# A conditioned attention block on one core: low parts of q and k made by GpSimd from a second eviction, two products of y at later slots

## The chip, the core and the metric

One Trainium2 chip, one of its cores, one launch. Times are microseconds of device time of that core. The kernel before takes 348.88 us (median of three runs, 348.82 to 350.72). TensorE multiplies, VectorE (DVE), ScalarE (ACT) and GpSimd (POOL) do elementwise work, and SyncE (SP) issues most DMAs; each runs its own stream of instructions in order, and they meet at semaphores.

## What is computed

Sixteen batches of 256 tokens with 256 features, sixteen heads of 16:

```python
h = _sln(hidden, w, ln_g, ln_b, Wg, bg, Wb, bb)       # gamma * LayerNorm + beta, gamma and beta from w
qkv = (h @ Wqkv.T + bqkv).reshape(B, N, num_heads, hd, 3)
energy = jnp.einsum('bhqd,bhkd->bhqk', q, k)
att = jax.nn.softmax(energy, axis=-1) / D ** 0.5
out = jnp.einsum('bhqk,bhkd->bhqd', att, v)
out = out @ Wp.T + bp
h1 = out + hidden
h2 = _sln(h1, w, ln_g, ln_b, Wg, bg, Wb, bb)
return h2 + h1
```

## The kernel before, in words

All products run as fp32r. To keep accuracy, an operand is split into a high part (rounded on eviction) and a low part (what the rounding lost), and a product is the sum of three: high by high, low by high, high by low. So q and k of a batch each exist twice in SBUF, as `qk_h` and `qk_l`, and SP's DMAs stack both in the partitions of `qst` and `kst`, so that one 128-deep matmul gives a head's full score.

**Steps and slots.** The work is pipelined over batches. Step b (b = -1 to 14) has 16 slots, one for each head h. In slot h TensorE makes the transposed scores of batch b (`scores`, tile st, two matmuls) and the scores of batch b + 1 from which only the row maxima are wanted (`scores_max`, tile sa, two matmuls). ACT takes the exponential of st into p (L602). DVE takes the row maxima of sa into mx (`maximum`, L688). Two banks each of st and sa alternate: `scores(b, h)` waits for the exponential of slot h - 2, `scores_max(b + 1, h)` for the maxima of slot h - 2. Between the scores stand, by slots that a table of constants at the top of the file gives, the projections of q and k of batch b + 2 (into banks m0 and m1, slots 0 to 6), v of b + 1 (m0, slots 7 and 8), the output projection of b - 1 (m1, slots 12 to 15), the products with v (`weigh`, 32 short matmuls, at slot 10 for heads 0 to 7 and at slot 2 of the next step for heads 8 to 15), and transposes. What is left after step 14 (the last scores, the last output) is written out as `last_step` and `finish`.

**The transpose of the maxima.** At slot 1 `transpose_max(b, 1, pv_ps[0])` (L1072) turns the maxima of heads 8 to 15 and writes into bank pv_ps[0]. That bank held the weighted values of heads 0 to 7, so TensorE first waits for `att_ready`, which DVE gives with `normalise(b - 1, 0, 1)` (L711, tile att), the last thing that DVE does in a step: the table `between` of DVE's `step` puts `normalise(b, 0, 0)` (L707, a reciprocal) in front of the maxima of slot 15 and `normalise(b, 0, 1)` behind them. In that table a key is (slot, side): side 0 stands in front of that slot's maxima, side 1 behind them.

**q and k.** ACT evicts the high parts: `high_q` in slot 5 (L522, two instructions of 128x256) and `high_k` in slot 7 (L532). DVE makes the low parts by `low_qk` (L723, two instructions for q behind the maxima of slot 5, two for k behind those of slot 7) straight from the PSUM bank: bank plus bias minus high part. `ql_ready` and `kl_ready` tell SP that the low parts may be sent and tell TensorE that the banks m0 and m1 are free again. Only for batch 1, in the first step, ACT writes a second, unrounded eviction (`full`, L631) into a free part of p32, and GpSimd subtracts (`low_full`, L415).

**The second LayerNorm.** `residual(b - 2, stage)` on DVE, stages 0 to 5: the sum h1, its statistics, and two products of y. Stage 4 (L804) is (h1 - mean) times gamma, stage 5 (L812) is that times rstd plus `h1b`; each is two instructions of 128x256 whose tensor inputs both lie in SBUF. GpSimd makes h1b (`add_beta`, L396), and adds the bias of the output projection to x for the next batch (`add_bias`, L387: xa plus bias_b, both in SBUF). `y_ready` releases SP's DMA of the output.

**GpSimd in a step**: DMAs of the negated maxima into qst (`maxima`, slots 3 and 11), a power for rstd (L430, slot 5), the normalisation of x for b + 3 (`norm_x`, L378, slot 5), `add_beta` (slot 6), the low part of h for b + 3 (`low_h`, L410, slot 12), then `add_bias` (slot 0 of the next step). It has no barrier at a slot; each instruction runs as soon as its semaphores allow.

**SP in a step**: the stack of b + 1, second half of the heads; x of b + 4; the stack of b + 2, first half (`send`: q high, q low, k high, k low, two DMAs each); gamma and beta of b - 1; the output of b - 2. `scores_max` waits for a stack at slots 0 and 8.

The functions that the change touches and what calls them:

Of the kernel before, what the change touches and what calls it, by code (L numbers as in the profile page):

```python
# [44 lines left out]
Q_SLOTS, K_SLOTS, V_SLOTS, P_SLOTS = (0, 1, 3, 4), (4, 5, 5, 6), (7, 7, 8, 8), (12, 13, 14, 15)  # L45
S_MT1, S_AT, S_MT0, S_XT = 1, 10, 9, 10
S_QH, S_KH, S_VH = 5, 7, 9
WARM = (10, 4, 4, 4)
V_FIRST = ((4, 5, 6, 6), (9, 10, 11, 12))
X_FIRST = 8  # L50
# [7 lines left out]
def cond_block(nc, x, condT, vectors, WgT, WbT, WqkvT, WpT, bp, out):  # L58
    gb_dram = nc.dram_tensor("gb_rows", (B, 2 * D), F32, kind="Internal").ap()
    with ExitStack() as ctx:  # L60
# [81 lines left out]
        stack_in = [[sem(f"stack_in{g}{p}") for p in range(2)] for g in range(2)]  # L142
        max_in = [[sem(f"max_in{g}{p}") for p in range(2)] for g in range(2)]
        max_first = sem("max_first")
        full_ready = sem("full_ready")
        qpad_ready = sem("qpad_ready")
        kpad_ready = sem("kpad_ready")
        y_out = [sem("y_out0"), sem("y_out1")]
# [207 lines left out]
        def _(pool):  # L356
# [54 lines left out]

            def low_full(a, t, ready):

                pool.wait_ge(full_ready, t + 1)
                pool.tensor_tensor(qk_l[:, par(a), t].rearrange("p g n -> p (g n)"), p32[:, H - 2 + t, :],  # L415
                                   qk_h[:, par(a), t].rearrange("p g n -> p (g n)"), ALU.subtract).then_inc(ready, 1)

            def step(b):
                for h in range(H):
                    if h == 5 and has(b):  # L420

                        one, two = has(b + 3), has(b - 2)
                        if one:
                            wait(pool, v_step, 3 * (b + 3) + 3)
                            wait(pool, xn_ready, 1 * (b + 3))
                        if two:
                            wait(pool, ln2_step, 4 * (b - 2) + 3)
                            wait(pool, y_ready, 1 * (b - 2))
                        which = slice(0 if one else 1, 2 if two else 1)
                        pool.tensor_tensor(rstd[:, which], vare[:, which], minus_half[:, which],  # L430
                                           ALU.pow).then_inc(rstd_ready, 1)
                    if first(b + 1) and h == 0:
                        low_full(1, 0, ql_ready)
                    if first(b + 1) and h == 5:
                        rstd_x(2)
                        low_full(1, 1, kl_ready)
                        norm_x(2)
                        pool.wait_ge(wph_ready, 1)
                        pool.tensor_tensor(wp_l[:], wp[:], wp_h[:], ALU.subtract).then_inc(wpl_ready, 1)
                    if h == 3:  # L440
                        maxima(b, 1)
                    if h == 11 and has(b):
                        maxima(b + 1, 0)
                    if h == 6 and has(b - 2):
                        add_beta(b - 2)
                    if h == 5 and has(b + 3) and has(b):
                        norm_x(b + 3)
                    if h == 0 and has(b - 1):
                        add_bias(b - 1)
                    if h in (13, 14) and b == B - 2:  # L450
                        add_bias(b + h - 13)
                    if h == 12:
                        low_h(b + 3)
# [42 lines left out]
        def _(act):  # L496
# [29 lines left out]
            def high_k(a):  # L526
# [6 lines left out]
                                             ACT.Identity, bias=vecs[:, 5, g:g + 1])  # L533
                o.then_inc(kh_ready, 1)

            def high_v(a, ps):

                wait(act, v_done, 1 * a + 1)
                wait(act, pv_done, 2 * (a - 1))
                nc.scalar.activation(v_st[:, par(a), :, :, 0:HD],  # L540
                                     ps[:].rearrange("p (t h d) -> p t h d", t=TT, h=H),
                                     ACT.Copy).then_inc(v_ready, 1)
# [9 lines left out]
            def step(b):  # L552
                for h in range(H):
# [5 lines left out]
                        high_q(b + 2)  # L559
                    if h == S_KH and not first(b + 1):  # L560
                        high_k(b + 2)
                    if h == S_MT1 + 1 and has(b):
                        high_max(b, 1, pv_ps[0])
                    if h == S_MT0 + 1 and has(b + 1):
# [60 lines left out]
                    act.dma_start(raw(kst[r:P:P // HD, 0, 0:HH, :]),  # L625
                                  raw(qk_h[:, 0, 1, 0, :])).then_inc(stack_in[0][0], 16)

            def full(a, t, ps):

                for g in range(KT):  # L630
                    o = nc.scalar.activation(p32[:, H - 2 + t, g * N:(g + 1) * N], ps[:, g * N:(g + 1) * N],  # L631
                                             ACT.Identity, bias=vecs[:, 4 + t, g:g + 1])
                o.then_inc(full_ready, 1)

            for dst, src, landed in ((wg, WgT, wg_in), (wb, WbT, wb_in)):
                act.dma_start(dst[:], src.rearrange("(k p) n -> p k n", p=P)).then_inc(landed, 16)
# [43 lines left out]
        def _(dve):  # L680
# [169 lines left out]
            def step(b):  # L850
# [5 lines left out]
                    (4, 0): [lambda: residual(b - 2, 2), lambda: norm1(b + 3, 0)],  # L856
                    (4, 1): [lambda: residual(b - 2, 3), lambda: norm1(b + 3, 1)],
                    (5, 0): [lambda: norm1(b + 3, 2)],
                    (5, 1): [lambda: low_qk(b + 2, 0, m0, qh_ready, ql_ready)],
                    (7, 0): [lambda: normalise(b - 1, 1, 0)],  # L860
                    (7, 1): [lambda: low_qk(b + 2, 1, m1, kh_ready, kl_ready)],
                    (8, 0): [lambda: normalise(b - 1, 1, 1)],
                    (9, 1): [lambda: residual(b - 2, 4)],
                    (11, 0): [lambda: low_max(b + 1, 0), lambda: low_att(b - 1), lambda: residual(b - 2, 5)],
                    (15, 0): [lambda: normalise(b, 0, 0)],
                    (15, 1): [lambda: normalise(b, 0, 1)],
                }
                if first(b + 1):
                    for slot in ((4, 0), (4, 1), (5, 0), (5, 1), (7, 1), (11, 0)):
                        del between[slot]  # L870
                    between[(9, 0)] = [lambda: low_max(0, 0)]
                for h in range(H):
# [94 lines left out]
        def _(pe):  # L967
# [278 lines left out]
            def step(b):  # L1246
                for h in range(H):
# [3 lines left out]
                    if h == (X_FIRST if first(b + 1) else S_XT) and has(b + 3):  # L1251
                        if has(b - 1):
                            wait(pe, v_ready, 1 * (b + 1) + 1)
                        elif has(b):
                            wait(pe, ql_ready, 1 * (b + 2) + 1)
                        else:
                            pe.wait_ge(full_ready, 1)
                        turn_x(b + 3)
                    if h == S_AT and has(b - 1):
                        turn_att(b - 1)  # L1260
# [17 lines left out]
                    for quarter in [n for n in range(4) if K_SLOTS[n] == h and has(b + 2) and not first(b + 1)]:  # L1278
                        if quarter == 0:
                            wait(pe, h1_ready, 1 * (b - 2) + 1)  # L1280
                            wait(pe, kl_ready, 1 * (b + 1) + 1)
                        project_qk(b + 2, 1, m1, k_done, quarter)
                    if h == S_MT0 and has(b + 1):
                        wait(pe, h1_ready, 1 * (b - 2) + 1)
                        wait(pe, kl_ready, B if not has(b + 2) else 1 * (b + 2) + 1 if has(b) else 1)
                        if first(b + 1):
                            pe.wait_ge(bias_ready, 1)
                        transpose_max(b + 1, 0, pv_ps[1] if first(b + 1) else m1)
                    for quarter in [n for n in range(4) if V_SLOTS[n] == h and has(b + 1) and has(b - 1)]:
                        if quarter == 0:  # L1290
                            wait(pe, ql_ready, (1 * (b + 2) + 1) if has(b + 2) else B)
                            wait(pe, v_ready, 1 * b + 1)
                        project_v(b + 1, m0, quarter)
                    for quarter in [n for n in range(4) if P_SLOTS[n] == h and has(b - 1)]:
                        if quarter == 0 and first(b - 1):
                            pe.wait_ge(wpl_ready, 1)
                        if quarter == 0:
                            wait(pe, aTl_ready, 1 * (b - 1) + 1)
                            wait(pe, h1_ready, 1 * (b - 2) + 1)
                            wait(pe, kl_ready, (1 * (b + 2) + 1) if has(b + 2) else B)  # L1300
                            wait(pe, ml_ready, 2 * min(b + 1, B - 1) + 1)
                        project_out(quarter)
                    if h < 4 and first(b + 1):
# [73 lines left out]
```

## Time and profile before

| | before |
|---|---|
| median of 3 runs | 348.88 us (348.82 to 350.72) |
| the profiled execution | 349.5 us, of which the span of its instructions is 347.7 us |
| busy: PE, PEld, DVE, ACT, POOL | 334.0, 288.6, 297.0, 242.8, 159.0 us |
| share of the span | 96%, 83%, 85%, 70%, 46% |
| DMA | 48.87 MB, mean 141 GB/s |
| granted TensorE clock, mean | 0.99 |
| chain that ended last | PE 86%, DVE 5%, ACT 2%, DMA 2%, POOL 2% |

PE is the matmul side of TensorE and PEld its loading of weights, which overlaps. Busy time of PE is modelled and matmuls are pipelined, so a busy PE says that something was always in flight, not that nothing waits. Lines such as L688 are lines of the kernel before.

### The profile page before, as it was taken

Reading aid. Unit: us, or ns where it says so; the run is one execution under the profiler, and the core shown is the slowest. Engines: PE = TensorE matmul, PEld = TensorE weight load, DVE = VectorE, ACT = ScalarE, POOL = GpSimd, SP = SyncE. Lnnn points to the kernel's source line nnn. Section 1 sums busy time; section 2 is a strip of 40 time slices with the busy share of each in tenths; the row PEclk is TensorE's granted clock in tenths of the full one; section 3 lists DMA queues with packets and bytes.
Section 4 is the critical chain, followed back from the end, with each engine's and each line's share of the span. In section 5 each row is a group of like instructions: output and inputs, shape, how many; then the busy total and the mean of one; then the engine's idle time right before and its main releaser. Section 6 shows DMA issues by size and latency. Waiting matters only on the chain.

```text
span 347.7 us, 8982 instructions
## 1 busy us (share of the span) xinstructions
PE 334.0 (96%) x3173; PEld 288.6 (83%) x3173; DVE 297.0 (85%) x728; ACT 242.8 (70%) x476; POOL 159.0 (46%) x187
## 2 busy tenths in 40 slices
PE   8886989999999999999999999999999999999993
PEld 4675968889898888888898888888898888888773
DVE  4874877789898989989898989989898988998684
ACT  7762686868678686868687686868687686766740
POOL 5476261525464462726454462726454453225330
PEclk9997899999999999999999999999999999999999
DMA  8487245544555465565545565656546454652011
GB/s 239 128 202 204 58 123 151 150 134 129 161 131 158 135 180 155 136 173 139 157 133 156 134 176 153 141 154 160 156 135 154 106 170 124 168 147 75 18 60 60
DMA packets 47705, 48.87 MB, mean 141 GB/s; under 512 B 6287, under 2 KB 41374, under 8 KB 47662
## 3 DMA queue, kind: packets, MB, share of 16 engines
q1 hardware_dynamic: 44782, 47.00, 49.3%
q0 software_dynamic: 1984, 0.51, 0.9%
q10 hardware_dynamic: 896, 0.80, 0.8%
q8 instruction: 25, 0.41, 0.5%
q14 instruction: 18, 0.15, 0.1%
HBM read 9.99 MB, written 4.23 MB: 41 GB/s over the span
## 4 chain that ended last, share of the span: by engine, by line
PE 86%; DVE 5%; ACT 2%; DMA 2%; POOL 2%; issue 2%; SPq 0%; DVEq 0%; POOLq 0%; ACTq 0%
PE m L969 24%; PE st L969 19%; PE sa L969 18%; PE pv L969 17%; PE pv L1058 4%; PE pv L1139 2%; PE m L1098 2%; DMA wqkv<-WqkvT_dram 2%; DVE mx L688 1%; DVE qk_l L723 1%; POOL qk_l L415 1%; POOL xn L378 1%; PE pv L1072 1%; PE m L1072 1%; ACT qk_h L522 0%
## 5 line engine op out<-in xcount | busy, mean ns | idle before, releaser
L688 DVE TENSOR_REDUCE mx<-sa 128x2 f32<-128x512 f32 x256 | 171.6, 683 | 30.1 <-PE sa L969 29.0
L602 ACT ACTIVATE p<-st 128x512 f32<-128x512 f32 x240 | 140.9, 598 | 38.0 <-PE st L969 33.9
L969 PE MATMUL sa<-kst,qst 126*128 126x256 f32 x512 | 106.5, 290 | 1.6 <-DVE mx L688 1.1
L969 PE MATMUL st<-qst,kst 128*128 128x256 f32 x496 | 104.0, 292 | 0.7 <-DMA qst<-m_l 0.5
L969 PEld LDWEIGHTS st<-qst,kst 128*128 128x128 f32 x496 | 75.1, 188 | 14.3 <-issue 12.8
L969 PEld LDWEIGHTS sa<-kst,qst 126*128 126x128 f32 x512 | 80.0, 193 | 3.8 <-DVE mx L688 2.1
L369 POOL DMA_DIRECT2D qst<-m_h x31 | 17.6, 566 | 117.0 <-DVE m_l L697 117.0
L969 PE MATMUL pv<-p,v_st 128*32 128x256 f32 x1008 | 61.0, 382 | 0.0
L969 PEld LDWEIGHTS pv<-p,v_st 128*32 128x32 f32 x1008 | 29.5, 109 | 21.0 <-ACT p L602 1.8
L969 PE MATMUL m<-hT_h,wqkv_h 128*128 128x256 f32 x128 | 36.8, 300 | 1.4 <-issue 0.8
L378 POOL TENSOR_SCALAR xn<-xa,mv,rstd 128x256 f32<-128x256 f32 x28 | 34.2, 1227 | 1.4
L969 PE MATMUL m<-hT_h,wqkv_l 128*128 128x256 f32 x128 | 34.4, 280 | 0.4 <-DVE wqkv_l L909 0.4
L969 PE MATMUL m<-hT_l,wqkv_h 128*128 128x256 f32 x128 | 34.2, 279 | 0.0
L430 POOL TENSOR_TENSOR rstd<-vare,minus_half 128x4 f32<-128x4 f32 (+1 forms) x15 | 14.2, 947 | 40.4 <-DVE vare L745 36.3
L550 ACT ACTIVATE oT<-pv 128x512 f32<-128x512 f32 x29 | 17.2, 594 | 21.6 <-PE pv L969 21.6
L723 DVE SCALAR_TENSOR_TENSOR qk_l<-m,vecs,qk_h 128x256 fp32r<-128x256 f32 x60 | 25.9, 473 | 0.6 <-ACT qk_h L522 0.6
L969 PEld LDWEIGHTS m<-hT_h,wqkv_h 128*128 128x128 f32 x128 | 23.5, 189 | 2.3 <-ACT wqkv_h L642 1.2
L969 PEld LDWEIGHTS m<-hT_h,wqkv_l 128*128 128x128 f32 x128 | 23.6, 190 | 0.6 <-DVE wqkv_l L909 0.6
L969 PEld LDWEIGHTS m<-hT_l,wqkv_h 128*128 128x128 f32 x128 | 23.4, 187 | 0.0
L396 POOL TENSOR_TENSOR h1b<-h,gb 128x512 f32<-128x512 f32 x15 | 19.3, 1289 | 6.9 <-DVE h L784 6.9
L387 POOL TENSOR_TENSOR xa<-xa,bias_b 128x512 f32<-128x512 f32 x16 | 20.6, 1292 | 0.0
L410 POOL TENSOR_TENSOR hT_l<-hT,hT_h 128x512 fp32r<-128x512 f32 x14 | 18.0, 1289 | 4.0 <-ACT hT_h L503 4.0
(149 smaller groups left out, 568.3 us busy)
## 6 DMA issues: line engine op xcount, KB each, us to landing
qst<-qk_h SPq DMA_DIRECT2D x64, 128.0 KB, 2.4
qst<-qk_l SPq DMA_DIRECT2D x64, 128.0 KB, 2.5
kst<-qk_l SPq DMA_DIRECT2D x64, 128.0 KB, 2.7
kst<-qk_h SPq DMA_DIRECT2D x62, 128.0 KB, 2.4
xa<-x_dram SPq DMA_DIRECT2D x16, 256.0 KB, 3.0
gb<-gb_rows SPq DMA_DIRECT2D x16, 256.0 KB, 3.9
out_dram<-y SPq DMA_DIRECT2D x15, 256.0 KB, 3.4
wqkv<-WqkvT_dram SPq DMA_DIRECT2D x1, 512.0 KB, 5.8
```

The source lines that it names most:

```text
L369: pool.dma_start(raw(qst[MAX_ROW + r:MAX_ROW + 1 + r, p, g * HH:(g + 1) * HH, :]) .rearrange("a h (t n) -> a (h t) n", t=TT), raw(m[:, g, ...
L378: o = pool.tensor_scalar(xn[:, t, :], xbuf(a)[:, t, :], mv[:, t, 0:1], rstd[:, 0, t:t + 1], ALU.subtract, ALU.mult)
L387: pool.tensor_tensor(xbuf(a), xbuf(a), bias_b[:].rearrange("p (a n) -> p a n", a=1).broadcast_to([P, TT, D]), ALU.add).then_inc(xdb_ready, 1)
L396: pool.tensor_tensor(h1b[:], h1[:], gb[:, par(a), D:2 * D].rearrange("p (a n) -> p a n", a=1) .broadcast_to([P, TT, D]), ALU.add).then_inc ...
L410: pool.tensor_tensor(hT_l[:, par(a)], hT[:], hT_h[:, par(a)], ALU.subtract).then_inc(hTl_ready, 1)
L430: pool.tensor_tensor(rstd[:, which], vare[:, which], minus_half[:, which], ALU.pow).then_inc(rstd_ready, 1)
L550: nc.scalar.activation(oT[:, g, :], pv_ps[g][:], ACT.Copy).then_inc(oT_ready, 1)
L602: nc.scalar.activation(p32[:, h, :], st_ps[h % 2][:], ACT.Exp).then_inc(exp_done, 1)
L688: dve.tensor_reduce(mx[:, par(a), h // HH, (h % HH) * TT:(h % HH + 1) * TT], sa_ps[h % 2][:].rearrange("p (t n) -> p t n", t=TT), AX.X, AL ...
L723: o = dve.scalar_tensor_tensor(out=qk_l[:, par(a), t, g, :], in0=ps[:, g * N:(g + 1) * N], scalar=vecs[:, 4 + t, g:g + 1], in1=qk_h[:, par ...
L969: return nc.tensor.matmul(o, l, r, start=start, stop=stop)
L1058: o = nc.tensor.transpose(pv_ps[g][:, t * N + c * P:t * N + (c + 1) * P], oT[:, g, c * N + t * P:c * N + (t + 1) * P], ident[:])
```

## The change

The low parts of q and k of all batches from 2 on are now made as those of batch 1 were. ACT evicts each bank a second time, unrounded and with its bias, q in slot 6 and k in slot 8, into `wg` and `wb` (weights that nothing reads after the set-up). GpSimd subtracts the high part from it: `low_full` of q at slot 6, behind `norm_x`; of k at slot 9; `add_beta` goes from slot 6 to slot 7 and so stands between the two. The four instructions of `low_qk` in each step leave DVE. The waits for the banks m0 and m1 are now for the second eviction (`fq_ready`, `fk_ready`) and no longer for the low part. Of the products of y, stage 4 goes from behind the maxima of slot 9 to behind those of slot 13, stage 5 from in front of slot 11 to behind slot 14.

```diff
+S_QF, S_KF = 6, 8
...
             def low_full(a, t, ready):
 
-                pool.wait_ge(full_ready, t + 1)
-                pool.tensor_tensor(qk_l[:, par(a), t].rearrange("p g n -> p (g n)"), p32[:, H - 2 + t, :],
+                if not has(a):
+                    return
+                pool.wait_ge((fq_ready, fk_ready)[t], 1 * a)
+                pool.tensor_tensor(qk_l[:, par(a), t].rearrange("p g n -> p (g n)"),
+                                   (wg, wb)[t][:].rearrange("p g n -> p (g n)"),
                                    qk_h[:, par(a), t].rearrange("p g n -> p (g n)"), ALU.subtract).then_inc(ready, 1)
...
-                    if h == 6 and has(b - 2):
+                    if h == 6 and has(b):
+                        low_full(b + 2, 0, ql_ready)
+                    if h == 7 and has(b - 2):
                         add_beta(b - 2)
+                    if h == 9 and has(b):
+                        low_full(b + 2, 1, kl_ready)
...
+            def full(a, t, ps):
+
+                if not has(a):
+                    return
+                wait(act, (ql_ready, kl_ready)[t], 1 * a)
+                for g in range(KT):
+                    o = nc.scalar.activation((wg, wb)[t][:, g, :], ps[:, g * N:(g + 1) * N],
+                                             ACT.Identity, bias=vecs[:, 4 + t, g:g + 1])
+                o.then_inc((fq_ready, fk_ready)[t], 1)
...
+                    if h == S_QF and not first(b + 1):
+                        full(b + 2, 0, m0)
+                    if h == S_KF and not first(b + 1):
+                        full(b + 2, 1, m1)
...
-                    (5, 1): [lambda: low_qk(b + 2, 0, m0, qh_ready, ql_ready)],
                     (7, 0): [lambda: normalise(b - 1, 1, 0)],
-                    (7, 1): [lambda: low_qk(b + 2, 1, m1, kh_ready, kl_ready)],
                     (8, 0): [lambda: normalise(b - 1, 1, 1)],
-                    (9, 1): [lambda: residual(b - 2, 4)],
-                    (11, 0): [lambda: low_max(b + 1, 0), lambda: low_att(b - 1), lambda: residual(b - 2, 5)],
+                    (11, 0): [lambda: low_max(b + 1, 0), lambda: low_att(b - 1)],
+                    (13, 1): [lambda: residual(b - 2, 4)],
+                    (14, 1): [lambda: residual(b - 2, 5)],
                     (15, 0): [lambda: normalise(b, 0, 0)],
                     (15, 1): [lambda: normalise(b, 0, 1)],
...
                         if quarter == 0:
                             wait(pe, h1_ready, 1 * (b - 2) + 1)
-                            wait(pe, kl_ready, 1 * (b + 1) + 1)
+                            wait(pe, fk_ready, 1 * (b + 1))
                         project_qk(b + 2, 1, m1, k_done, quarter)
...
                         if quarter == 0:
-                            wait(pe, ql_ready, (1 * (b + 2) + 1) if has(b + 2) else B)
+                            wait(pe, fq_ready, min(b + 2, B - 1))
                             wait(pe, v_ready, 1 * b + 1)
                         project_v(b + 1, m0, quarter)
```

The transpose of the maxima at slot 9 into m1 and the output projection likewise wait for `fk_ready` where they waited for `kl_ready`.

What stands in a row on DVE, from the maxima of slot 10 to those of slots 0 to 2 of the next step. Before:

```order
L697 SCALAR_TENSOR_TENSOR m_l<-m,m_h 16x128
L773 TENSOR_TENSOR aT_l<-pv,aT_h 128x512
L812 SCALAR_TENSOR_TENSOR y<-y,rstd,h1b 128x256 x2
L688 TENSOR_REDUCE mx<-sa 128x2 x4
L707 RECIPROCAL rec<-pv 128x16
L688 TENSOR_REDUCE mx<-sa 128x2
L711 TENSOR_TENSOR att<-pv,rec 128x2x128
L688 TENSOR_REDUCE mx<-sa 128x2 x3
```

The four maxima (mx<-sa) in a row are those of slots 11 to 14, the one behind rec that of slot 15. The same place after the change (lines are those of the changed file; L705 is the maxima, L724 rec, L728 att):

```order
L714 SCALAR_TENSOR_TENSOR m_l<-m,m_h 16x128
L790 TENSOR_TENSOR aT_l<-pv,aT_h 128x512
L705 TENSOR_REDUCE mx<-sa 128x2 x3
L821 SCALAR_TENSOR_TENSOR y<-h,mv,gb 128x256 x2
L705 TENSOR_REDUCE mx<-sa 128x2
L829 SCALAR_TENSOR_TENSOR y<-y,rstd,h1b 128x256 x2
L724 RECIPROCAL rec<-pv 128x16
L705 TENSOR_REDUCE mx<-sa 128x2
L728 TENSOR_TENSOR att<-pv,rec 128x2x128
```

Both pairs of y now stand between the maxima of slot 13 and the att of the step's end; before, neither did.

GpSimd through one step, from the power for rstd to the bias of x. Before:

```order
L430 TENSOR_TENSOR rstd<-vare,minus_half 128x4
L378 TENSOR_SCALAR xn<-xa,mv,rstd 128x256 x2
L396 TENSOR_TENSOR h1b<-h,gb 128x512
L369 DMA qst<-m_h 1x16x128
L369 DMA qst<-m_l 1x16x128
L410 TENSOR_TENSOR hT_l<-hT,hT_h 128x512
L387 TENSOR_TENSOR xa<-xa,bias_b 128x512
```

The same stretch after the change:

```order
L435 TENSOR_TENSOR rstd<-vare,minus_half 128x4
L380 TENSOR_SCALAR xn<-xa,mv,rstd 128x256 x2
L419 TENSOR_TENSOR qk_l<-wg,qk_h 128x512
L398 TENSOR_TENSOR h1b<-h,gb 128x512
L419 TENSOR_TENSOR qk_l<-wb,qk_h 128x512
L371 DMA qst<-m_h 1x16x128
L371 DMA qst<-m_l 1x16x128
L412 TENSOR_TENSOR hT_l<-hT,hT_h 128x512
L389 TENSOR_TENSOR xa<-xa,bias_b 128x512
```

Two subtractions of 128x512 have come in ahead of the DMAs of the maxima, the low part of h and the bias of x.

## Rows read from the trace of the kernel before

**Rows 1.** Busy time by engine in two consecutive stretches of 19.5 us, with instruction counts

```profile
131.95:151.45 19.50, 19.50 (x197) 17.29 (x196) 17.84 (x45) 14.58 (x30) 9.37 (x10) 1.00 0.54 151
151.45:170.95 19.50, 19.50 (x197) 17.29 (x196) 17.84 (x45) 14.58 (x30) 9.38 (x10) 1.00 0.54 152
```

**Rows 2.** The chain that ended last, one piece in step 0: start, us, what

```profile
42.84 0.78 DVE qk_l L723 x2
```

**Rows 3.** Groups by line and shape: count, busy us, mean ns, idle before

```profile
L602 ACT ACTIVATE p<-st 128x512 f32<-128x512 f32 x240 | 140.9, 598 | 38.0 <-PE st L969 33.9
...
L723 DVE SCALAR_TENSOR_TENSOR qk_l<-m,vecs,qk_h 128x256 fp32r<-128x256 f32 x60 | 25.9, 473 | 0.6 <-ACT qk_h L522 0.6
...
L415 POOL TENSOR_TENSOR qk_l<-p,qk_h 128x512 fp32r<-128x512 f32 x2 | 2.6, 1294 | 1.9 <-ACT p L631 1.9
...
L631 ACT ACTIVATE p<-m,vecs 128x256 f32<-128x256 f32 x4 | 1.7, 480 | 0.0
```

**Rows 4.** Timeline of DVE, slots 9 to 15 of one step: start, us, instruction

```profile
162.53 0.87 DVE L804 SCALAR_TENSOR_TENSOR y<-h,mv,gb 128x256 f32<-128x256 f32 x2
163.32 0.68 DVE L688 TENSOR_REDUCE mx<-sa 128x2 f32<-128x512 f32 x1
...
166.02 2.01 DVE L688 TENSOR_REDUCE mx<-sa 128x2 f32<-128x512 f32 x3 [0.42 <-PE sa L969]
168.20 0.69 DVE L688 TENSOR_REDUCE mx<-sa 128x2 f32<-128x512 f32 x1 [0.17 <-PE sa L969]
168.81 0.24 DVE L707 RECIPROCAL rec<-pv 128x16 f32<-128x16 f32 x1
169.47 0.69 DVE L688 TENSOR_REDUCE mx<-sa 128x2 f32<-128x512 f32 x1 [0.42 <-PE sa L969]
170.08 0.41 DVE L711 TENSOR_TENSOR att<-pv,rec 128x256 f32<-128x256 f32 x1
```

**Rows 5.** Timeline of PE, slot 1 of the step after it

```profile
170.69 0.40 PE L969 MATMUL sa<-kst,qst 126*128 126x256 f32 x2
170.92 0.28 PE L1072 MATMUL pv<-ident,mx 128*128 128x128 f32 x1
```

**Rows 6.** Timelines of POOL and DVE: two additions of POOL, one pair of L804

```profile
167.00 1.29 POOL L387 TENSOR_TENSOR xa<-xa,bias_b 128x512 f32<-128x512 f32 x1
...
337.24 1.27 POOL L491 TENSOR_TENSOR xn<-xa,gb 128x512 f32<-128x512 f32 x1
...
338.13 1.06 DVE L804 SCALAR_TENSOR_TENSOR y<-h,mv,gb 128x256 f32<-128x256 f32 x2
```

**Rows 7.** Timelines of POOL, ACT and PE within the same step

```profile
158.85 2.44 POOL L378 TENSOR_SCALAR xn<-xa,mv,rstd 128x256 f32<-128x256 f32 x2
...
164.49 0.61 POOL L369 DMA_DIRECT2D qst<-m_h  x1 [1.95 <-DVE m_l L697]
...
159.11 0.84 ACT L532 ACTIVATE qk_h<-m,vecs 128x256 fp32r<-128x256 f32 x2 [0.45 <-PE m L969]
...
161.74 0.48 PE L969 MATMUL st<-qst,kst 128*128 128x256 f32 x2
162.07 0.50 PE L969 MATMUL sa<-kst,qst 126*128 126x256 f32 x2
```

**Rows 8.** DMA issues: x count, KB each, median us from issue to landing

```profile
kst<-qk_l SPq DMA_DIRECT2D x64, 128.0 KB, 2.7
```

**Rows 9.** Timelines at the ends of steps 13 and 14: DVE, PE, POOL

```profile
302.07 2.00 DVE L688 TENSOR_REDUCE mx<-sa 128x2 f32<-128x512 f32 x3
306.60 0.31 PE L1072 MATMUL pv<-ident,mx 128*128 128x128 f32 x1
...
319.13 1.99 DVE L688 TENSOR_REDUCE mx<-sa 128x2 f32<-128x512 f32 x3
...
319.16 2.54 POOL L387 TENSOR_TENSOR xa<-xa,bias_b 128x512 f32<-128x512 f32 x2
...
323.16 0.41 DVE L711 TENSOR_TENSOR att<-pv,rec 128x256 f32<-128x256 f32 x1
```

More of the change, by code:

```diff
@@ L144, in cond_block @@
         max_first = sem("max_first")
-        full_ready = sem("full_ready")
+        fq_ready = sem("fq_ready")
+        fk_ready = sem("fk_ready")
         qpad_ready = sem("qpad_ready")
@@ L626, in high_k0 @@
                                   raw(qk_h[:, 0, 1, 0, :])).then_inc(stack_in[0][0], 16)
[L628 to L633, printed above, removed]
             for dst, src, landed in ((wg, WgT, wg_in), (wb, WbT, wb_in)):
@@ L868, in step @@
                 if first(b + 1):
-                    for slot in ((4, 0), (4, 1), (5, 0), (5, 1), (7, 1), (11, 0)):
+                    for slot in ((4, 0), (4, 1), (5, 0), (11, 0)):
                         del between[slot]
@@ L1254, in step @@
                         elif has(b):
-                            wait(pe, ql_ready, 1 * (b + 2) + 1)
+                            wait(pe, fq_ready, 1 * (b + 2))
                         else:
-                            pe.wait_ge(full_ready, 1)
+                            pe.wait_ge(fq_ready, 1)
                         turn_x(b + 3)
@@ L1284, in step @@
                         wait(pe, h1_ready, 1 * (b - 2) + 1)
-                        wait(pe, kl_ready, B if not has(b + 2) else 1 * (b + 2) + 1 if has(b) else 1)
+                        if has(b):
+                            wait(pe, fk_ready, min(b + 2, B - 1))
+                        else:
+                            pe.wait_ge(kl_ready, 1)
                         if first(b + 1):
@@ L1299, in step @@
                             wait(pe, h1_ready, 1 * (b - 2) + 1)
-                            wait(pe, kl_ready, (1 * (b + 2) + 1) if has(b + 2) else B)
+                            wait(pe, fk_ready, min(b + 2, B - 1))
                             wait(pe, ml_ready, 2 * min(b + 1, B - 1) + 1)
```

## Prediction

> **What bounds the kernel now.** I read the views in this order. First the busy time of each engine in two stretches that lie exactly one step apart: both are 19.50 us, with the same 197 matmuls, PE busy for all of 19.50 and DVE for 17.84 [rows 1]. So the middle of the run repeats to the hundredth, its period is 19.50 us, and the engine without a gap is TensorE. Second the chain of waits that ended last: it is 86% PE, and DVE's work on q and k shows in it as a piece of the first full step, 42.84 us [rows 2]. Third, for the change, the groups by line, which give the price of each operation [rows 3], and last the timelines, which say who is how far behind whom at the two places where work comes and goes. What the reader should see before any sum: with TensorE the bound, work taken off DVE gives back only what TensorE now loses waiting for DVE, which in the steady part is next to nothing, while work put in front of something that TensorE waits for costs from the point where its slack is used up.
>
> **That slack, at the end of a step.** At slot 1 TensorE transposes the maxima into the bank that DVE's last product of the step (att, L711) still reads. att starts at 170.08 and takes 0.41, so it ends at 170.49 [rows 4]; the transpose starts at 170.92 [rows 5]. The slack is 0.43 us. DVE gets there from the three maxima of slots 11 to 13, which end at 168.03; then it waits 0.17 for the scores of slot 14 and 0.42 for those of slot 15 [rows 4], so 0.59 of idle time also lies in this stretch.
>
> **Part 1: y moved to slots 13 and 14.** Two pairs of 128x256 products come into this stretch. A pair takes 0.87, and the next instruction starts 0.79 after it (162.53 to 163.32); a maximum passes on after 0.61 (168.20 to 168.81), because an instruction starts about 0.08 before the one ahead of it has ended, so the reciprocal of 0.24 passes on after 0.16 [rows 4]. New times, in the frame of that step: the maxima of slots 11 to 13 end at 168.03 as before, since they wait for TensorE; stage 4 starts at 167.95, the maxima of slot 14 at 168.74, stage 5 at 169.35, the reciprocal at 170.14, the maxima of slot 15 at 170.30, att at 170.91, and att ends at 171.32. There is no wait left between them. With 0.05 us for the semaphore (an estimate; bounds 0 and 0.1) the transpose starts at 171.37 in place of 170.92: 0.45 us later. A part of these 0.45 us TensorE already loses one instruction earlier: its scores for the maxima of slot 1, at 170.69 [rows 5], need the maxima of slot 15, which end at 170.99, so 0.35 is waited there and the other 0.10 at the transpose; they don't add. DVE is level with TensorE again by slot 11, in front of whose maxima it stands idle for 0.42 [rows 4], so the delay is paid once per step and does not pile up.
>
> **A slower stage 4.** Stage 4 now starts at 167.95, and GpSimd's addition of the bias to x ran at 167.00 to 168.29 before [rows 6]. It moves later: two subtractions of 1.29 [rows 3] go in between norm_x, which ends at 161.29, and the DMAs of the maxima; they pass on after some 1.26 each, 2.5 in all, and GpSimd was idle for 1.95 in front of the first DMA [rows 7], which leaves 0.55; behind the DMAs it waits for ACT's hT_h, where a little more can be made up, so I take the addition to start 0.4 later, at 167.4, and to end at 168.7. It overlaps stage 4 by 0.75 (by 0.34 if it didn't move, by 0.87 at the most). What an overlap costs the trace shows once: the pair of L804 at 338.13 took 1.06 in place of 0.87, and a GpSimd addition ran until 338.51, so of 0.38 us beside it 0.19 were lost [rows 6]. At that rate 0.75 costs 0.37; the bounds are 0 and 0.43. The stall becomes 0.45 + 0.37 = 0.82 us.
>
> The Trainium skill (GPSIMD Engine Reference, Key points) says that GpSimd shares its SBUF interfaces with VectorE and that it contends with DVE instructions that have two SBUF inputs. Stage 4 has two (h1 and gamma), the maxima and low_qk have one or none in SBUF; the one pair at 338.13 agrees. By this rule the result is the forecast below, without it the first rival.
>
> **How often.** Stages 4 and 5 run in steps 2 to 14. For the 11 steps 2 to 12 the stall is 0.82: 9.0 us. Step 13: GpSimd has neither norm_x nor the low part of h there, so its addition is over before; the maxima end at 304.07, and the same sums (0.79, 0.61, 0.79, 0.16, 0.61, 0.41, less the first 0.08) end att at 307.36, against a transpose that started at 306.60 [rows 9]: 0.81. Step 14: the maxima end at 321.12, additions run on GpSimd until 321.70, so stage 4 loses 0.33, and att ends at 324.74 where it ended at 323.57 and was already waited for [rows 9]: 1.17. Together 11.0 us.
>
> **Part 2: low_qk off DVE.** 56 instructions (14 batches of 4, the other 4 of the 60 are batch 0's) of 0.473 leave: 26.5 us of DVE [rows 3], all beside a busy TensorE except in step 0, where they are on the chain: two pairs, 1.6 us at the most [rows 2]. There the same step gets ACT's second evictions and later DMAs, and TensorE's own work is close behind; I take 0.5 us of gain, bounds 0 and 1.6. In the steady steps TensorE's pair for the maxima of slot 10 takes 0.50 against 0.40 elsewhere [rows 5, 7], which I read as a wait of 0.1 for DVE; it goes: at the most 12 times 0.1 = 1.2 us.
>
> **Part 3: the second eviction on ACT.** 56 instructions of 0.48 [rows 3], 27 us, four in a step. ACT has gaps, but not everywhere. From 159.11 it evicts k (0.84) [rows 7], then comes exponential 7 (0.60) [rows 3], then the new pair (0.84, as k's), then exponential 8 (0.60). Less 0.11 by which one starts inside the one before (two of 0.473 take 0.84), exponential 8 ends at 161.66, and TensorE's scores of slot 10, which wait for it, start at 161.74 [rows 7]. That is just in time. Without overlaps it would be 161.99 and cost 0.3 a step, 3.6 us; I take 0.05 a step against the 0.1 won above, net -0.05 times 12 = -0.6 us (bounds -1.2 and +3.6).
>
> **Part 4: the subtractions on GpSimd.** 28 of 1.29 [rows 3], 36 us, on an engine that is half idle. Behind them wait SP's DMAs of the low parts. q's ends at about 162.6, k's at 165.1, so the last two DMAs of the stack are issued from 165.1; the second leaves an issue later, some 0.6 (GpSimd's own issue in rows 7 takes 0.61), and lands 2.7 after that, at 168.4 [rows 8]. TensorE wants it at slot 0 of the next step, not before 169.5 (170.69 less a slot, 19.5/16). 1.1 us spare: cost 0. SP's output DMA now waits for stage 5 until about 170.6, and the second half of the next stack is queued behind it, about 1 us later than before; it is wanted at slot 8: cost 0.
>
> **The sum** is made against the profiled execution: 349.5 + 11.0 - 0.5 - 0.6 = 359.4 us, 9.9 more. That execution is 0.6 above the median of 348.88, so on the median: 358.8 us.
>
> **The rivals.**
> - No contention: stage 4 beside GpSimd's addition is no slower. For it: the evidence is one pair. Then 11 times 0.45 + 0.81 + 0.84 - 1.1 = 5.5, 354.4 us.
> - DVE is relieved and nothing is lost. The mechanism: DVE is 3.2 us a step lighter ahead of the maxima of slot 11 (two pairs of q and k, two of y, 0.79 each), arrives early at slot 14, and att still ends before TensorE needs its bank. It decides at one point, att's end against 170.87. Then the gains stand alone: 1.2 + up to 1.6, so 346.1 to 348. Against it: the maxima of slots 11 to 13 wait for TensorE, so being early doesn't carry over [rows 4].
> - GpSimd late: if its subtractions run 2 us later than worked out, the low part of k lands after slot 0 is due, by more than the 0.82 that are lost anyway, and each further 0.5 us costs 12 times 0.5: about 365. The idle stretch of 1.95 speaks against it.
> - ACT late at slot 10 by the full 0.3: 0.35 more in 12 steps, 363.0.
>
> **How the numbers follow.** Chances: forecast 0.58, no contention 0.22, GpSimd late 0.04, ACT late 0.06, relief 0.10 (of it 0.03 for faster by over 1%, since its best price is 0.8%, and 0.07 for within 1%). One per cent is about what a measurement of this kernel tells from no change. Slower by over 1%, above 352.4: 0.90. The range takes in the first rival with 1 us below it and the forecast with most of ACT's bound above: 353.5 to 362.5.
>
> **What would show it.** In the changed profile: a period of 20.2 to 20.3 us (19.50 + 0.82 - 0.05); a new wait of TensorE at the slot 1 transpose for DVE's att and at slot 1's scores for the maxima of slot 15; pairs of L804's successor at about 1.2 us and of L812's at 0.87; no DVE idle time between slots 13 and 15. A period of 19.95 with pairs of 0.87 would be the first rival. It is wrong if the period stays at 19.5, or if TensorE's new waits stand elsewhere: at slot 0 for a DMA, at slot 10 for ACT.

## The result, and the profile after

The changed kernel takes 361.56 us (median of 4 runs, 360.82 to 362.39) against 348.85 for the kernel before (4 runs): ratio 1.036, 95% interval 1.033 to 1.039. It is 12.7 us slower; 9.9 were forecast. The profiled execution took 362.23 us, with a span of 360.4.

The windows of two consecutive steps of the changed kernel, to be held against [rows 1] (columns: stretch, its length, then busy us and count of PE, PEld, DVE, ACT, POOL, the granted clock, the DMA share, GB/s):

```profile
147.67:168.10 20.43, 19.93 (x198) 17.37 (x202) 17.05 (x41) 15.78 (x33) 11.80 (x13) 1.00 0.52 145
168.10:188.53 20.43, 19.93 (x198) 17.37 (x202) 17.05 (x41) 15.78 (x33) 11.80 (x13) 1.00 0.54 145
```

The period has gone from 19.50 to 20.43 us, and PE is no longer busy throughout. DVE does less (17.05 after 17.84), ACT and POOL do more (15.78 after 14.58, 11.80 after 9.37). So DVE, the busiest engine behind TensorE, was relieved, and the step became longer all the same: the time went into waits.

Where, the timeline of DVE at the end of a step says, which answers to [rows 4]:

```profile
170.67 2.00 DVE L705 TENSOR_REDUCE mx<-sa 128x2 f32<-128x512 f32 x3 [1.21 <-PE sa L985]
172.59 1.47 DVE L821 SCALAR_TENSOR_TENSOR y<-h,mv,gb 128x256 f32<-128x256 f32 x2
173.99 0.68 DVE L705 TENSOR_REDUCE mx<-sa 128x2 f32<-128x512 f32 x1
174.59 0.87 DVE L829 SCALAR_TENSOR_TENSOR y<-y,rstd,h1b 128x256 f32<-128x256 f32 x2
175.38 0.24 DVE L724 RECIPROCAL rec<-pv 128x16 f32<-128x16 f32 x1
175.54 0.62 DVE L705 TENSOR_REDUCE mx<-sa 128x2 f32<-128x512 f32 x1
176.09 0.40 DVE L728 TENSOR_TENSOR att<-pv,rec 128x256 f32<-128x256 f32 x1
```

From the maxima of slots 11 to 13 to att nothing waits any more; the 1.21 us of idle time lie in front of the row and are of no use to it. Beside it POOL, and then PE at slots 0 and 1, which answer to [rows 6] and [rows 5]:

```profile
172.09 1.28 POOL L389 TENSOR_TENSOR xa<-xa,bias_b 128x512 f32<-128x512 f32 x1
```

```profile
174.26 0.39 PE L985 MATMUL st<-qst,kst 128*128 128x256 f32 x2
174.81 0.47 PE L985 MATMUL sa<-kst,qst 126*128 126x256 f32 x2 [0.16 <-DVE mx L705]
...
175.48 0.40 PE L985 MATMUL st<-qst,kst 128*128 128x256 f32 x2
176.22 0.51 PE L985 MATMUL sa<-kst,qst 126*128 126x256 f32 x2 [0.34 <-DVE mx L705]
176.56 0.31 PE L1088 MATMUL pv<-ident,mx 128*128 128x128 f32 x1
```

The rows before that these are held against, beside [rows 5]:

```profile
169.86 0.40 PE L969 MATMUL sa<-kst,qst 126*128 126x256 f32 x2
170.45 0.40 PE L969 MATMUL st<-qst,kst 128*128 128x256 f32 x2
```

A pair sa starts 0.24 after its pair st where nothing is waited for (170.45 and 170.69 before). Here it is 0.55 at slot 0 and 0.74 at slot 1, and the transpose comes 0.34 after it in place of 0.23: 0.31 + 0.50 + 0.11 = 0.92 us. What stands behind a late pair comes later too: from sa of slot 0 to the next st it is 0.67 (174.81 to 175.48) in place of 0.59 (169.86 to 170.45), and from the transpose to the weighing of slot 2 it is 1.07 in place of 1.03. So the stall is 1.04 us. It is more than the 0.93 of the period, because the step gets 0.12 back, 0.10 of it at TensorE's pair sa of slot 10, which took 0.50 before [rows 7] and is 0.40 now:

```profile
166.82 0.40 PE L985 MATMUL sa<-kst,qst 126*128 126x256 f32 x2
```

For the whole: 11 steps times 0.93 are 10.2 us. From transpose to transpose at slot 1, step 13 takes 19.37 (299.15 to 318.52; before 287.94 to 306.60, 18.66) and step 14 17.80 (318.52 to 336.32; before 17.03): 0.7 and 0.8. The other 1.1 lie in front of the first weighing of step 0, at 48.29 against 47.20 before. Nothing shows that they belong to the change: in executions whose programs are the same up to there the first weighing starts at 46.2 to 48.6 us (46.24 in e5_y_apart, 48.58 in e3_bias_late), which is a wider spread than 1.1.

### The profile page after: what moved, and what is told of

Read it like the earlier page. It is cut to its first block, busy times and chain, and to the rows that moved or that the text cites. A ratio compares the mean times of both kernels' runs of the same rounds, so it can differ in the third digit from the quotient of the medians.

```text
span 360.4 us, 8996 instructions
## 1 busy us (share of the span) xinstructions
PE 341.4 (95%) x3173; PEld 291.6 (81%) x3173; DVE 284.2 (79%) x672; ACT 259.6 (72%) x532; POOL 193.3 (54%) x215
## 4 chain that ended last, share of the span: by engine, by line
PE 70%; DVE 14%; issue 9%; ACT 3%; POOL 2%; DVEq 0%; POOLq 0%; ACTq 0%
PE m L985 18%; PE pv L985 17%; PE sa L985 15%; PE st L985 13%; DVE mx L705 6%; DVE y L821 3%; DVE y L829 3%; PE pv L1074 2%; PE m L1114 2%; PE pv L1155 2%; ACT p L625 1%; POOL qk_l L419 1%; ACT qk_h L531 1%; PE pv L1088 1%; POOL xn L380 1%
## 5 line engine op out<-in xcount | busy, mean ns | idle before, releaser
L705 DVE TENSOR_REDUCE mx<-sa 128x2 f32<-128x512 f32 x256 | 170.6, 683 | 45.7 <-PE sa L985 41.8
L985 PEld LDWEIGHTS sa<-kst,qst 126*128 126x128 f32 x512 | 79.1, 190 | 13.2 <-DVE mx L705 8.6
L985 PE MATMUL m<-hT_h,wqkv_h 128*128 128x256 f32 x128 | 37.6, 309 | 0.6 <-ACT hT_h L639 0.6
L985 PEld LDWEIGHTS m<-hT_h,wqkv_h 128*128 128x128 f32 x128 | 24.7, 201 | 1.6 <-issue 1.6
L419 POOL TENSOR_TENSOR qk_l<-wg,qk_h 128x512 fp32r<-128x512 f32 x15 | 19.4, 1290 | 1.5 <-ACT wg L551 1.5
L419 POOL TENSOR_TENSOR qk_l<-wb,qk_h 128x512 fp32r<-128x512 f32 x15 | 19.3, 1285 | 1.5 <-ACT wb L551 1.5
```

The lines of the kernel that those rows point to most:

```text
L705: dve.tensor_reduce(mx[:, par(a), h // HH, (h % HH) * TT:(h % HH + 1) * TT], sa_ps[h % 2][:].rearrange("p (t n) -> p t n", t=TT), AX.X, AL ...
L985: return nc.tensor.matmul(o, l, r, start=start, stop=stop)
```

## The experiments

Each kernel was timed beside the kernel before; the ratios are to that. "Late addition" below means GpSimd's addition of the bias to x moved from slot 0 to slot 3.

**e1_y_back.** The second part of the change undone:

```diff
+                    (9, 1): [lambda: residual(b - 2, 4)],
-                    (11, 0): [lambda: low_max(b + 1, 0), lambda: low_att(b - 1)],
-                    (13, 1): [lambda: residual(b - 2, 4)],
-                    (14, 1): [lambda: residual(b - 2, 5)],
+                    (11, 0): [lambda: low_max(b + 1, 0), lambda: low_att(b - 1), lambda: residual(b - 2, 5)],
```

> The changed kernel with the two products of y back at their old places (stage 4 behind the maxima of slot 9, stage 5 in front of slot 11); ACT's second eviction and GpSimd's subtractions stay. Theory (the whole loss is DVE's longer row in front of att at the end of a step): period 19.40 to 19.50 us, no wait of TensorE at slots 0 and 1, 348 to 350 us. The pair of stage 4 may still be slow (over 1.1 us in place of 0.87), since it now stands beside GpSimd's subtraction, but there it costs nothing. Rival (a part of the loss is the second eviction on ACT or the later low parts): period above 19.6, 352 us or more.

Measured: 366.18 us, ratio 1.050 (1.047 to 1.053), period 20.99. It is slower still, and by more than the rival expected. The expectation had foreseen that the pair of stage 4 could be slow here, but at no cost. The timelines of DVE, POOL and PE in one step:

```profile
167.67 2.96 DVE L821 SCALAR_TENSOR_TENSOR y<-h,mv,gb 128x256 f32<-128x256 f32 x2
170.55 0.68 DVE L705 TENSOR_REDUCE mx<-sa 128x2 f32<-128x512 f32 x1
171.15 0.27 DVE L714 SCALAR_TENSOR_TENSOR m_l<-m,m_h 16x128 fp32r<-16x128 f32 x1
171.35 0.67 DVE L790 TENSOR_TENSOR aT_l<-pv,aT_h 128x512 fp32r<-128x512 f32 x1
171.94 0.86 DVE L829 SCALAR_TENSOR_TENSOR y<-y,rstd,h1b 128x256 f32<-128x256 f32 x2
...
167.65 1.27 POOL L398 TENSOR_TENSOR h1b<-h,gb 128x512 f32<-128x512 f32 x1
168.88 1.47 POOL L419 TENSOR_TENSOR qk_l<-wb,qk_h 128x512 fp32r<-128x512 f32 x1
...
170.86 0.40 PE L984 MATMUL st<-qst,kst 128*128 128x256 f32 x2
171.28 0.50 PE L984 MATMUL sa<-kst,qst 126*128 126x256 f32 x2
172.07 0.39 PE L984 MATMUL m<-wp_h,aT_h 128*128 128x256 f32 x1 [0.29 <-DVE aT_l L790]
...
172.53 0.39 PE L984 MATMUL st<-qst,kst 128*128 128x256 f32 x2
173.46 0.50 PE L984 MATMUL sa<-kst,qst 126*128 126x256 f32 x2 [0.54 <-DVE mx L705]
```

The pair of stage 4 takes 2.96 us where it took 0.87. It runs beside h1b and the new subtraction until 170.35, 2.68 us, and loses 2.09. Behind it aT_l and the maxima come late, and TensorE waits at slots 12 and 13: sa starts 0.42 and 0.93 after its st in place of 0.24, and the output projection starts 0.79 after the first sa in place of 0.24 (166.07 to 166.31 before). These three make 1.42 of the 1.61 us by which the period exceeds 19.38. (One step in this trace took 22.39; there the DMA of the maxima landed 5.04 us after its issue, and the period is read from the others.) So the place of y in the kernel before is only good as long as GpSimd has nothing to do beside it; with the subtractions there, moving y gains 4.6 us (366.18 to 361.56).

**e2_y_only.** The kernel before with only the products of y moved (the same lines of the table as in the change, no second eviction, low_qk still on DVE).

> The kernel before with only the two products of y moved to behind slots 13 and 14; low parts of q and k stay on DVE. Theory: GpSimd's addition to x runs earlier than in the changed kernel (167.0 to 168.3 in the frame of the trace of before), overlaps stage 4 by some 0.3 us only, and costs some 0.25 us of it; with the 0.45 of the bare row the period is 20.1 to 20.2 us and the time 356 to 359 us. Rival (the loss comes mostly from ACT's and GpSimd's new work): under 354 us.

Measured: 357.14 us, ratio 1.026 (1.022 to 1.031), period 20.08. The time is as expected, the period at the lower edge, since stage 4 lost 0.14 and not 0.25. The pair and the addition beside it:

```profile
169.31 1.01 DVE L804 SCALAR_TENSOR_TENSOR y<-h,mv,gb 128x256 f32<-128x256 f32 x2
...
168.36 1.29 POOL L387 TENSOR_TENSOR xa<-xa,bias_b 128x512 f32<-128x512 f32 x1
```

They overlap by 0.34 us, and the pair loses 0.14.

**e3_bias_late.** The changed kernel with nothing of GpSimd beside stage 4:

```diff
-                    if h == 0 and has(b - 1):
+                    if h == 3 and has(b - 1):
                         add_bias(b - 1)
```

> The changed kernel with GpSimd's addition of the bias to x moved from slot 0 to slot 3, behind the DMAs of the maxima, so that nothing of GpSimd runs beside stage 4. Theory (contention of two instructions with two SBUF inputs each): the pair of stage 4 takes 0.87 us in place of 1.47, TensorE waits 0.4 us a step at slots 0 and 1 in place of 1.0, period 19.8 to 19.9, time 354.5 to 356 us. Rival (stage 4 is slow at that place for another reason, as SP's or GpSimd's DMAs): pair 1.4 us or more, 361 us.

Measured: 355.03 us, ratio 1.017 (1.014 to 1.021), period 19.83. The pair:

```profile
170.47 0.87 DVE L821 SCALAR_TENSOR_TENSOR y<-h,mv,gb 128x256 f32<-128x256 f32 x2
...
177.21 1.30 POOL L389 TENSOR_TENSOR xa<-xa,bias_b 128x512 f32<-128x512 f32 x1
```

One addition, moved on an engine that is half idle, takes 0.60 out of the period, all that the pair was too long. The contention is shown, and by its removal. In this trace one late transfer is hidden behind the row: in the step that ends at 154.02 the low part of k landed at 152.75 and TensorE's sa of slot 0 started 0.46 after its st.

**e4_y5_late.** The changed kernel with stage 4 back behind slot 9 and stage 5 behind slot 14.

> The changed kernel with stage 4 back behind slot 9 and only stage 5 behind slot 14. Theory (the row in front of att has 0.59 us of idle time and 0.43 of slack, which hold one pair of 0.79 but not two): att ends just before TensorE asks for its bank, period 19.40 to 19.55, time 348 to 350.5 us. Rival (any product of y in the row costs its own 0.79 us): period about 20.2, 357 us.

Measured: 362.41 us, ratio 1.040 (1.036 to 1.043), period 20.63. It told nothing of the row in front of att, since it has e1's fault: stage 4 took 2.96 us again, and stage 5 met the addition and took 1.40. e6 and e7 ask the same question without that.

**e5_y_apart.** Stage 4 beside norm_x, stage 5 where it was:

```diff
+                    (6, 1): [lambda: residual(b - 2, 4)],
-                    (11, 0): [lambda: low_max(b + 1, 0), lambda: low_att(b - 1)],
-                    (13, 1): [lambda: residual(b - 2, 4)],
-                    (14, 1): [lambda: residual(b - 2, 5)],
+                    (11, 0): [lambda: low_max(b + 1, 0), lambda: low_att(b - 1), lambda: residual(b - 2, 5)],
```

> The changed kernel with stage 4 of y behind slot 6, where GpSimd runs norm_x (one tensor input in SBUF), and stage 5 back in front of slot 11, after GpSimd's subtraction of k. Theory (only GpSimd instructions with two SBUF tensor inputs slow a product of y down; second evictions and subtractions cost nothing by themselves): the pair of stage 4 takes 0.87 to 0.95 us beside norm_x, stage 5 at most 1.3, period 19.40 to 19.50, 347 to 349 us, so no slower than before and perhaps 0.2% faster. Rival (anything that GpSimd does slows y): the pair of stage 4 takes 2 us or more, and TensorE waits for the maxima of slots 6 and 7: 355 us or more.

Measured: 354.58 us, ratio 1.015 (1.012 to 1.018). The period is 19.38, below that of the kernel before, as the theory had it; the total is not. (The profiled execution is one of the shorter ones, 352.59.) The pairs in a middle step, and then stage 5 in step 14:

```profile
163.19 1.34 DVE L829 SCALAR_TENSOR_TENSOR y<-y,rstd,h1b 128x256 f32<-128x256 f32 x2
...
176.87 1.01 DVE L821 SCALAR_TENSOR_TENSOR y<-h,mv,gb 128x256 f32<-128x256 f32 x2
...
318.50 3.77 DVE L829 SCALAR_TENSOR_TENSOR y<-y,rstd,h1b 128x256 f32<-128x256 f32 x2
```

```profile
162.58 1.28 POOL L419 TENSOR_TENSOR qk_l<-wb,qk_h 128x512 fp32r<-128x512 f32 x1
...
176.80 2.70 POOL L380 TENSOR_SCALAR xn<-xa,mv,rstd 128x256 f32<-128x256 f32 x2
...
319.06 2.52 POOL L389 TENSOR_TENSOR xa<-xa,bias_b 128x512 f32<-128x512 f32 x2
```

Beside norm_x, whose instructions have one tensor input, the pair loses only 0.14 in its whole length, and norm_x loses too (2.70 against the 2.44 of [rows 7]). In the last two steps GpSimd has no norm_x, so its later work comes beside stage 4 (in step 13 the subtraction of q and h1b, in step 14 h1b), and its additions beside stage 5, one in step 13 and two in step 14; there the pairs take 1.61 to 3.77 us, and steps 13 and 14 take 20.87 and 19.96 us where the kernel before needs 18.66 and 17.03. That is 5.1 us lost in two steps.

**e6_one_pair.** Stage 4 behind slot 6, stage 5 behind slot 14, late addition: one undisturbed pair in the row.

> The changed kernel with stage 4 behind slot 6, stage 5 behind slot 14 and GpSimd's addition of the bias at slot 3: one pair in the row in front of att, with nothing of GpSimd beside it. Theory: 0.59 us of idle time and 0.43 of slack hold the pair of 0.79, no wait of TensorE at slot 1, period 19.40 to 19.55, 347.5 to 350 us. Rival (each pair in the row costs what it takes): period about 20.2.

Measured: 350.80 us, ratio 1.004 (1.002 to 1.007), period 19.38, the last two steps 19.98 and 17.85. No wait at slot 1 in the middle steps: the row in front of att holds one pair. The total is 0.8 above what was expected: the last two steps, where stage 4 again meets the subtraction and h1b (2.51 us) or h1b alone (1.61), lose 1.3 and 0.8. Step 2 takes 19.81, because TensorE waits there at slot 0 for the low part of k.

**e7_before_y5.** The kernel before with only stage 5 behind slot 14.

> The kernel before with only stage 5 moved to behind slot 14; stage 4 stays behind slot 9. Theory: as with one pair in the changed kernel, the row holds it: period 19.40 to 19.55, 348 to 350 us. If the row had less room than worked out, the period is above 19.7 and the time above 351.

Measured: 349.75 us, ratio 1.003 (1.001 to 1.005), period 19.50, last two steps 18.90 and 17.29. The same answer without any other edit; only in steps 13 and 14, whose slack is smaller, some 0.25 us each are lost.

**e8_before_bias.** e2 with the late addition: both pairs in the row, undisturbed, without second eviction and subtractions.

> The kernel before with both products of y behind slots 13 and 14 and GpSimd's addition of the bias at slot 3; low parts stay on DVE. Theory (second eviction and subtractions cost nothing of their own): the same 19.80 to 19.87 us of period and 354 to 356 us as the changed kernel with the late addition. Rival (they have a cost of their own, from ACT at slot 10 or the late low parts): this kernel is faster than that one, by 1.5 us or more.

Measured: 354.86 us, ratio 1.017 (1.014 to 1.020), period 19.94. The time is as expected and the same as that of e3 (355.03), with a period 0.11 longer than e3's and 0.07 above what was expected. So at the places of the changed kernel ACT's second eviction and GpSimd's subtractions, together with the relief of DVE that they bring, cost nothing in a usual step; they gain 0.11. What they did use up is the time in hand of the low part of k. Its last transfer landed 2.3 to 3.7 us before TensorE's sa of slot 0 in the kernel before, over eleven steps of the middle, and 0.5 to 1.8 us before it in the changed kernel, where that sa is itself 0.3 late.

**e9_best.** e5, with the last steps as in e1, where both pairs had been undisturbed:

```diff
                     (6, 1): [lambda: residual(b - 2, 4)],
...
+                if b >= B - 3:
+                    between[(9, 1)] = between.pop((6, 1))
```

> The kernel with stage 4 behind slot 6 and stage 5 in front of slot 11, except that from step 13 on, where GpSimd has no norm_x and subtracts beside slot 6, stage 4 stands behind slot 9 again. Theory: both pairs are 0.87 us again in steps 13 and 14, these steps take 18.6 and 17.1 us in place of 20.9 and 20.0, the others 19.38 as they did; the time is 346.5 to 348.5 us, 0.1 to 0.6% below the kernel before. Rival (the rest of the 354.6 us has another cause than these two steps): 351 us or more.

Measured: 349.12 us (12 runs) against 349.30 (17 runs) for the kernel before on the same chip, ratio 0.997 (0.994 to 1.000). Steps 13 and 14 take 18.59 and 17.03 as expected, the others 19.38 but for one. The time itself is outside the expected range; the runs lie in two groups, 346.6 to 347.4 and 349.1 to 349.7, most likely because the starts differ between executions by more than the gain. The ratio is inside, but its interval reaches 1.000, so it is the period that shows the gain and not the time. Two windows of it:

```profile
132.26:151.64 19.38, 19.33 (x193) 16.98 (x193) 16.99 (x40) 15.65 (x34) 12.07 (x12) 1.00 0.51 138
151.64:171.02 19.38, 19.38 (x196) 17.22 (x195) 16.98 (x40) 15.32 (x34) 12.06 (x12) 1.00 0.58 166
```

In the second TensorE is without a gap again, now at 19.38. That is 0.12 us a step, 1.4 us in 12 steps, as far as these runs show all that relieving DVE gives here. In the first it has a short one. The chain of waits shows the transfer of the low part of k, and behind it TensorE's pair of slot 0:

```profile
148.44 2.62 DMA kst<-qk_l
...
151.10 0.51 PE sa L986 x2
```

That step, from transpose to transpose, takes 19.70. One step like it is in e5 (19.55) and in e6 (19.81). So with the low parts on GpSimd their transfer has next to nothing in hand, and now and then it costs 0.2 to 0.4 us.

**Six periods from the same terms.** Without these waits a step takes 19.38 us with the low parts on GpSimd and 19.50 with them on DVE. Two pairs of y in the row cost 0.45, as the forecast had it, and the contention comes on top. (e1 and e4, where stage 4 delays slots 12 and 13, are not of this form.)

| kernel | base | row | lost by stage 4 | sum | measured |
|---|---|---|---|---|---|
| changed kernel | 19.38 | 0.45 | 0.60 | 20.43 | 20.43 |
| e3_bias_late | 19.38 | 0.45 | 0 | 19.83 | 19.83 |
| e2_y_only | 19.50 | 0.45 | 0.14 | 20.09 | 20.08 |
| e8_before_bias | 19.50 | 0.45 | 0 | 19.95 | 19.94 |
| e6_one_pair | 19.38 | 0 (one pair) | out of the row | 19.38 | 19.38 |
| e7_before_y5 | 19.50 | 0 (one pair) | none | 19.50 | 19.50 |

## Why the prediction was right, and where it was off

**Right: the mechanism and its place.** TensorE had no gap, so that DVE's relief could give little; the slack in front of the transpose of slot 1 was 0.43 us, and two pairs of y overrun it. TensorE's new waits stand at slot 1, for the maxima and at the transpose, as foretold. A third, of 0.31 at slot 0 for the maxima of slot 14, was not in the forecast; it is there because stage 4, which stands in front of these maxima, took longer than was worked out, and in e3, without the contention, that pair starts 0.23 after its st (172.15 to 172.38).

**Right to a hundredth: 0.45 for the bare row.** e3 and e8 measure it alone: 19.83 less 19.38, 19.94 less 19.50. That it fits so closely is in part luck, since the 0.05 in it for the semaphore was a guess; from att's end to the transpose it is 0.07 here (176.49 to 176.56).

**Mis-sized: the slower stage 4.** The step that failed is "at that rate 0.75 costs 0.37; the bounds are 0 and 0.43". The overlap was right (0.78 us, 172.59 to 173.37), the rate was not: 0.60 were lost, beyond the bound. The rate came from one short meeting, 0.19 lost in 0.38 [rows 6]. The runs give, as overlap and loss: 0.34 and 0.14, 0.38 and 0.19, 0.67 and 0.47 (e5, stage 5), 0.71 and 0.54 (e4, stage 5), 0.78 and 0.60, 0.93 and 0.74 (e5, stage 4 of step 14). Where the pair meets one such instruction the loss is the overlap less 0.17 to 0.20, and not a share of it; 0.19 in 0.38 looked like half by accident of its length. The traces say it in another way too: a product of y that is slowed by an addition or subtraction of this kind ends 0.28 to 0.30 us after that instruction has ended, in every trace, however long the overlap was. In e1 both products of the pair meet one, hence 2.09 lost in 2.68. By this the forecast's own overlap of 0.75 would have cost 0.56. The upper bound was drawn from the same single point and so was no bound.

The stall was 1.05 in place of 0.82: 0.23 a step, 2.5 us over 11 steps. Against the profiled execution the forecast was 2.8 short, and the other terms make up the rest: the start, 1.25 us later at the transpose of step 0's slot 1 (39.27 after 38.02), was in no term; step 0 gained 0.35 less than was put; against these stand 0.8 more of gain in steps 1 to 12, and 0.1 and 0.4 less loss in steps 13 and 14. That the time is still in the range, 0.9 under its upper end, is luck: that end was set for a late ACT, which did not happen, and not for this term.

**The Trainium skill** (GPSIMD Engine Reference, Key points) was right in kind: contention with DVE instructions that have two SBUF inputs. The runs agree and put numbers to it, and they add that GpSimd's side matters: beside its instructions with one tensor input (norm_x) the loss is 0.14 us over the whole pair (1.01 us).

**Right in total, by too narrow an argument: parts 3 and 4 at nothing.** e3 against e8 shows that second eviction and subtractions cost nothing in a usual step at the places of the changed kernel. The 1.1 us in hand that the forecast gave the low part of k is in the middle of what is measured (0.5 to 1.8), but it was one step's figure: it differs from step to step, and in one step each of e5, e6 and e9 it is gone. But the forecast priced only what waits for the subtractions, and not what runs beside them: in e1 they cost 19.38 to 20.99, 1.6 us a step. So the move of y, which the forecast took as the sole cause of the loss, is at the same time what keeps the other half of the change from doing worse. The comparison "low parts moved, y left" stood in no part of the working.

**The small terms.** The gain at slot 10 was put at 0.1 a step with 0.05 given back by ACT; the period gains 0.12 with nothing given back (ACT's chain was in time, as worked out). Step 0 was put at 0.5 of gain. The chain of waits in it now reads

```profile
42.07 0.84 ACT qk_h L531 x2
42.91 0.49 ACT p L625
43.40 0.73 ACT wg L551 x2
44.13 0.49 ACT p L625
44.62 0.73 ACT qk_h L541 x2
45.35 0.49 ACT p L625
45.84 0.73 ACT wb L551 x2
46.57 0.50 ACT p L625
```

ACT has taken DVE's place on it: what q and k took off DVE in [rows 2] came back as two pairs of ACT, and the gain in this step is 0.15. Step 13 was put at 0.81 and is 0.7. Step 14 was put at 1.17 and is 0.8, since GpSimd's additions there ended just before stage 4 began, in place of running 0.66 into it:

```profile
332.96 0.87 DVE L821 SCALAR_TENSOR_TENSOR y<-h,mv,gb 128x256 f32<-128x256 f32 x2
...
330.31 2.56 POOL L389 TENSOR_TENSOR xa<-xa,bias_b 128x512 f32<-128x512 f32 x2
...
336.32 0.33 PE L1088 MATMUL pv<-ident,mx 128*128 128x128 f32 x1 [0.92 <-DVE att L728]
```

**The rivals.** No contention: refuted, e3 has the time that this rival gives. Relief of DVE and nothing lost: it is true of the middle steps of e5, e6 and e9, that is, where at most one pair is in the row and nothing slows stage 4; the point at which it decides, att's end, was the right one. GpSimd late: not in the changed kernel, and in one step each of e5, e6 and e9, at 0.2 to 0.4 us. ACT late: it did not show.

## What to carry to other kernels

Where one engine has no gap, a change to the others is priced by the slack in front of what it waits for, and idle time counts only if it lies inside the row between two meetings with that engine: here 1.21 us in front of the row were worth nothing, and 0.59 in it plus 0.43 behind it held one pair of 0.79 but not two. When work is given to GpSimd, look first at which DVE instructions with two inputs in SBUF run beside it, and only then at who waits for it. A price taken from a single meeting of two engines is a point and not a rate: two meetings of different length tell whether the loss is a share of the overlap or the overlap less a constant.

## What the runs showed of the hardware that was not expected

- A DVE instruction with two tensor inputs in SBUF stands still beside a GpSimd instruction of that kind, all but 0.17 to 0.20 us of a meeting: 0.60 lost in 0.78, and with two meetings 2.09 in 2.68, a pair of 128x256 products going from 0.87 to 2.96 us. GpSimd hardly notices (1.47 in place of 1.29 at the most). A meeting of only 0.10 us cost nothing (0.87 in e7 at 259.21). Beside a GpSimd instruction with one tensor input the same pair lost 0.14 in its whole length (e5). The maxima, whose input is in PSUM, and aT_l, with one input in each memory, kept their times beside the same GpSimd instructions (0.67 to 0.69).
- In step 14 of e5 the pair took 3.77 us, 2.90 more than alone, while the additions beside it ran for 2.52. In step 13 it took 2.55, 1.68 more than alone, beside 1.30 of addition. In both the first product, 0.47 alone, began 0.56 before the addition and should have ended in front of it, but ended 0.28 to 0.29 after the last addition. What stands beside it before the addition is GpSimd's DMA issue of the maxima (until 319.05), which in e1 did not slow the same pair (0.86 at 171.94). What makes the difference stays open.
- Starts of programs that are the same up to there differ by some 2 us, which is more than the gain of e9. A difference of a few tenths of a per cent is better read from the period of a step than from the time.
